# A per-token modulation repeated over rows: selection-matrix products against a store to DRAM and a strided read back

## The chip, the cores and the metric

The kernel runs on one core of a Trainium2 chip. The metric is the device time of one execution in microseconds; lower is better. Five engines work side by side: TensorE (PE, matrix products), VectorE (DVE), ScalarE (ACT), GpSimd (POOL) and SyncE (SP), which in this kernel only issues transfers. ACT issues transfers too, on a queue of its own. Engines wait for each other and for transfers through semaphores.

## The reference

Eight sequences of 1024 tokens with 512 channels go through two residual layers. The first is an adapter of rank 128 with a layer norm. The second is the one that matters here:

```
ctx    = causal_ema(x, tau_ctx)
gated  = x * sigmoid([x, ctx] @ Wg.T + bg)
h1     = gelu(x @ Wn1.T + bn1)
mod    = 0.5 + sigmoid(h1 @ Wn2.T + bn2)          # per token: D = 8 numbers
traces = [causal_ema(gated * mod[..., d], tau_d) for d in range(8)]
temporal = sum over d of traces[d] * softmax(blend)[d]
out    = (gelu(x @ Wsoma.T + b) * sigmoid(temporal @ Wtemp.T + b)) @ Wout.T
x      = x + layernorm(out)
```

The eight traces are decaying sums over time. Each scales the gated input of a token by one of the eight numbers `mod` of that token.

## The kernel before

The 8192 tokens are 16 tiles of 512 (`TOK`), each of four blocks `b` of 128 tokens. A program of slots runs over them: slot k finishes tile k-1 (its gates and output product), works on the middle of tile k, and begins tile k+1. Each engine's program is written out by hand in the order in which the engine runs it; only semaphores tie the engines together. A wait therefore holds everything behind it on that engine.

All large products are made three times with rounded operands (high times high, high times low, low times high), so PE has a great deal to do: L1026 is the line of these products.

The decaying sums inside a tile are made in spans of 32 tokens. For a block, `within_spans` (L1217 on PE) multiplies a table `Arep` with `U`, both with 128 partitions that stand for 32 tokens times four of the eight traces (NQ = 4; the two halves of the eight are `hh`, NH = 2). So `U` needs the gated input `g` with every token repeated on four partitions. [...] DVE then multiplies what was read by the blend weights (`products`, L902; 16 per tile, numbered 0 to 15 in the text). The first block waits for its four reads (`grep_in0`).

`Arep` (L962 on DVE) is the power of the decay times the modulation, so it needs the modulation repeated on the same partitions, `m_rep`: 16 spans times NH numbers on each partition. The modulation `m_nat` (L937, L588, L944) has a token per partition. Before the change it is repeated in three steps: PE multiplies it with a 0/1 selection matrix `spread` (`spread_modulation`, L1189; the matrix lies in `T_sb1`, which other data need in between, so SP loads it anew for each tile at L357); DVE keeps of each four columns the one that belongs to the partition by a product with `own` (L955) and a sum over four (L958). L911 is `gated`, which makes `g` ready.

The order around the change in one slot is, on PE: value gate 0, modulation, value gate 1, `spread_modulation`, value gates 2 and 3, half of a soma product, `within_spans` of block 0, and so on; on ACT: open gate 0, sigmoid of `m_nat`, store block 0, open gate 1, store block 1, and so on; on SP: load of the selection matrix, four output stores, `repeat_spans(0)` to `(3)`.

Of the kernel before, what the change touches and what calls it, by code (L numbers as in the profile page):

```python
# [4 lines left out]
P = 128  # L5
BATCHES, SEQ, C = 8, 1024, 512
# [34 lines left out]
def cond_resid_kernel(nc, x, xc, own, spread, ids, w1, w2, b1, b2, g0, be0, wg, wn1, wsoma, wtemp, wout, wn2,  # L41
# [10 lines left out]
    with ctx:  # L52
        def sb(name, shape, dt=F):
            return ctx.enter_context(nc.sbuf_tensor(name, shape, dt))
# [10 lines left out]
        def sem(name):  # L65
# [57 lines left out]
        m_all = U[:, 3, NI - 1, 96:96 + NI * NB * D].rearrange("p (y q) -> p y q", q=NQ)  # L123
# [6 lines left out]
        columns = sb("columns", [P, 11 + NQ])  # L130
        col, alpha_ctx, b1_col, own_q = columns[:, 0:9], columns[:, 9:10], columns[:, 10:11], columns[:, 11:11 + NQ]
# [8 lines left out]
        g_dram = nc.dram_tensor("g_blocks", [NB, P, C], F, kind="Internal").ap()  # L140
        x1_dram = nc.dram_tensor("x1_tiles", [2, P, NB * C], F, kind="Internal").ap()
# [31 lines left out]
        ld_spread = sem("ld_spread")  # L173
# [7 lines left out]
                 "m": 1, "mrep": 1, "S": 1, "Uused": PIECES // 2, "T": 4, "carry": 1}  # L181
# [22 lines left out]
        m_pre, m_ready, Bm_ready, mrep_ready, A_ready = sem("m_pre"), sem("m_ready"), sem("Bm_ready"), sem("mrep_ready"), sem("A_ready")  # L204
        mall_ready = sem("mall_ready")
# [85 lines left out]
        def _(sp):  # L291
# [26 lines left out]
            def first_loads():  # L318
# [5 lines left out]
                sp.dma_start(own_q, own).then_inc(ld_small, 16)  # L324
# [24 lines left out]
            def slot(k):  # L349
                has_prev, has_cur, has_next = parts_of(k)  # L350

                def load_spread():
                    if has_next:
                        sp.wait_ge(full["y"], upto(4, k + 1, NB - 1))
                    else:
                        sp.wait_ge(full["tt"], upto(4, k - 1, NB - 1))
                    sp.dma_start(T_sb1[:, :], spread).then_inc(ld_spread, 16)  # L357
# [16 lines left out]
                if has_prev:  # L374
# [11 lines left out]
                    if has_cur:  # L386
                        load_spread()
# [91 lines left out]
        def _(act):  # L479
# [6 lines left out]
            def slot(k):  # L486
# [95 lines left out]
                if has_cur:  # L582
# [44 lines left out]
            act.wait_ge(ld_small, 112)  # L627
# [14 lines left out]
        def _(dve):  # L642
# [16 lines left out]
            def small_tables():  # L659

                dve.wait_ge(ld_small, 112)
# [712 lines left out]
```

## Time and profile before

| | |
|---|---|
| Median of 3 runs | 1344.43 us (1341.11 to 1346.19) |
| The profiled execution | 1347.22 us, of which the span from first to last instruction is 1345.4 us |
| Busy share of ACT, POOL | 41%, 34% |
| Granted TensorE clock | 0.995 of full speed |
| Transfers | 190.41 MB in 93933 packets, a mean of 142 GB/s |
| Queue of ACT's transfers (q10) | 16.78 MB, 3.3% of 16 engines |

The profile counts an engine as busy while an instruction runs. Products on PE overlap, and their ends are modelled: a long row of them starts one each 0.227 us, though each is shown as 0.39 us. A busy PE is therefore no proof that PE is what the end waits for. "PEld" is PE's loading of weights. A row of the timeline is an instruction or several alike: its start, its length, its engine, its line, what it writes and reads, how many; in brackets the idle time before it and what ended that.

### The profile page before, as it was taken

To read this page: it belongs to the slowest core of one execution; us is meant where nothing else is said; L and a number is where in the kernel's file an instruction comes from. 1 tells how busy PE (TensorE), PEld (TensorE's weight loads), DVE (VectorE), ACT (ScalarE), POOL (GpSimd) and SP (SyncE) were. 2 spreads that over 40 slices of the span, in tenths; PEclk is the share of its full clock that TensorE was granted. 3 is DMA by queue.
4 is the path that set the end of the run, shared out by engine and by line. 5 is a ranking of instruction groups with operands and counts; after the bars stand their busy time and mean duration, and the time that the engine had idled before them with its cause. 6 is when DMAs were issued, how large, how long until landed. Compare 5 with 4: busy or idle time off the path is not lost.

```text
span 1345.4 us, 19282 instructions
## 1 busy us (share of the span) xinstructions
PE 1305.6 (97%) x7580; PEld 1015.1 (75%) x7580; DVE 1044.1 (78%) x1542; ACT 555.0 (41%) x892; POOL 460.9 (34%) x364
## 2 busy tenths in 40 slices
PE   4899999999999999999999999999999999999997
PEld 2668778687787878778687787878868787787766
DVE  7988777797778877787787778778687787778575
ACT  3426253343624525254252634426254262534422
POOL 3407144061521606135061531606125061431102
PEclk9899999999999999999999999999999999999999
DMA  7372442715336171352715425173342714325150
GB/s 269 141 241 81 153 161 71 258 40 183 137 105 218 55 244 62 128 196 80 239 40 179 173 86 204 48 235 118 118 165 78 256 66 164 149 86 181 40 181 32
DMA packets 93933, 190.41 MB, mean 142 GB/s; under 512 B 10258, under 2 KB 14994, under 8 KB 89746
## 3 DMA queue, kind: packets, MB, share of 16 engines
q1 hardware_dynamic: 84626, 172.39, 37.7%
q10 hardware_dynamic: 9216, 16.78, 3.3%
q8 instruction: 60, 0.98, 0.3%
q14 instruction: 31, 0.25, 0.1%
HBM read 138.81 MB, written 50.33 MB: 141 GB/s over the span
## 4 chain that ended last, share of the span: by engine, by line
PE 58%; DVE 16%; issue 9%; DMA 7%; ACT 4%; SPq 2%; POOL 1%; DVEq 0%; POOLq 0%
PE ring L1026 40%; DVE U_f L902 7%; PE Tp L1217 5%; DMA g_blocks<-g_f 4%; PE Tp L1026 3%; PE Tp L1228 3%; DMA grep<-g_blocks 3%; SPq L371 2%; DVE stats L837 2%; PE ring L1242 2%; ACT U_f L561 2%; DVE g_f L911 1%; DMA x<-g_blocks 1%; PE ring L1060 1%; PE ring L1063 1%
## 5 line engine op out<-in xcount | busy, mean ns | idle before, releaser
L425 POOL TENSOR_TENSOR Arep_r<-W,Arep_r 128x512 fp32r<-128x512 f32 x14 | 18.2, 1297 | 541.9 <-ACT Arep_r L524 541.9
L902 DVE TENSOR_TENSOR U_f<-grep,w_qs 128x1024 f32<-128x1024 f32 x128 | 150.8, 1220 | 49.2 <-issue 45.2
L571 ACT ACTIVATE g_f<-g_f 128x512 f32<-128x512 f32 x64 | 40.5, 632 | 260.7 <-DVE g_f L907 260.5
L1217 PE MATMUL Tp<-U_f,Arep_f 128*32 128x256 f32 x2048 | 130.0, 384 | 5.5 <-DVE U_f L902 5.3
L452 POOL TENSOR_TENSOR grep_f<-grep_f,beta_row 128x512 f32<-128x512 f32 x64 | 82.1, 1320 | 68.1 <-DMA grep_f<-x_tiles 68.1
L1217 PEld LDWEIGHTS Tp<-U_f,Arep_f 128*32 128x32 f32 x2048 | 56.1, 109 | 65.2 <-DVE U_f L902 23.0
L1026 PE MATMUL ring<-x1T_hi,Wsoma_hi 128*128 128x512 f32 x256 | 103.4, 404 | 0.0
L1026 PE MATMUL ring<-Wg_hi,x1T_hi 128*128 128x512 f32 x256 | 103.3, 403 | 0.0
L1026 PE MATMUL ring<-seq_hi,Wtemp_hi 128*128 128x512 f32 x256 | 101.0, 394 | 0.1
L1026 PE MATMUL ring<-Wout_hi,g_r 128*128 128x512 f32 x256 | 99.9, 390 | 1.1 <-DVE soma_r L758 1.0
L1026 PE MATMUL ring<-Wg_hi,x1T_lo 128*128 128x512 f32 x256 | 100.2, 392 | 0.0
L1026 PE MATMUL ring<-x1T_hi,Wsoma_r 128*128 128x512 f32 x256 | 100.2, 391 | 0.0
L1026 PE MATMUL ring<-x1T_lo,Wsoma_hi 128*128 128x512 f32 x256 | 100.0, 391 | 0.0
L907 DVE TENSOR_TENSOR g_f<-ring,bg_row 128x512 f32<-128x512 f32 x64 | 44.1, 689 | 71.9 <-PE ring L1026 71.6
L1026 PE MATMUL ring<-seq_hi,Wtemp_r 128*128 128x512 f32 x256 | 99.8, 390 | 0.0
L1026 PE MATMUL ring<-seq_lo,Wtemp_hi 128*128 128x512 f32 x256 | 99.8, 390 | 0.0
L1026 PE MATMUL ring<-Wout_hi,soma_r 128*128 128x512 f32 x256 | 99.7, 390 | 0.0
L1026 PE MATMUL ring<-Wg_r,x1T_hi 128*128 128x512 f32 x256 | 99.7, 390 | 0.0
L1026 PE MATMUL ring<-Wg_hi,seq_hi 128*128 128x512 f32 x256 | 99.7, 389 | 0.0
L1026 PE MATMUL ring<-Wout_r,g_r 128*128 128x512 f32 x256 | 99.7, 389 | 0.0
L1026 PE MATMUL ring<-Wg_hi,seq_lo 128*128 128x512 f32 x256 | 99.7, 389 | 0.0
L1026 PE MATMUL ring<-Wg_r,seq_hi 128*128 128x512 f32 x256 | 99.7, 389 | 0.0
(185 smaller groups left out, 3192.8 us busy)
## 6 DMA issues: line engine op xcount, KB each, us to landing
grep<-g_blocks SPq DMA_DIRECT2D x128, 256.0 KB, 3.7
grep_f<-in_xc SPq DMA_DIRECT2D x16, 1024.0 KB, 7.8
grep<-in_x SPq DMA_DIRECT2D x16, 1024.0 KB, 9.3
x_tiles<-x SPq DMA_DIRECT2D x16, 1024.0 KB, 6.9
g_blocks<-g_f ACTq DMA_DIRECT2D x64, 256.0 KB, 3.5
grep_f<-g_blocks SPq DMA_DIRECT2D x64, 256.0 KB, 3.5
x<-g_blocks SPq DMA_DIRECT2D x64, 256.0 KB, 3.9
grep_f<-x_tiles SPq DMA_DIRECT2D x16, 1024.0 KB, 4.8
```

Of the source, the lines that this page charges most:

```text
L371: sp.dma_start(spans_of(k, b)[q:P:NQ, :, :], g_dram[b].rearrange("(i s) c -> s i c", i=NI)).then_inc(spans_in(k, b)[0], 16)
L425: nc.gpsimd.tensor_tensor(W1_split[:, 1, :, :], W1[:, :, :], W1_split[:, 0, :, :].bitcast(F), ALU.subtract).then_inc(w1lo_ready, 1)
L452: nc.gpsimd.tensor_tensor(x1_back[:, b, :], x1_back[:, b, :], beta1_row[:, :], ALU.add).then_inc(x1b_ready, 1)
L561: nc.scalar.activation(res[:, b, :], res[:, b, :], ACT.Identity, scale=rstd1[:, b:b + 1]).then_inc(scaled_ready, 1)
L571: nc.scalar.activation(g[:, b, :], g[:, b, :], ACT.Sigmoid).then_inc(sig_ready, 1)
L837: V_.bn_stats(stats0[:, b, :], new[:, b, :]).then_inc(ln0_step, 1)
L902: V_.tensor_tensor(U[:, (n + 2) % 4, :, :], spans_of(k, b)[:, :, at], w_qs[:, hh, at].unsqueeze(1).to_broadcast([P, NI, HC]), ALU.mult).th ...
L907: V_.tensor_tensor(g[:, b, :], bank_of("wg", k, b)[:, :], bg_row[:, :], ALU.add).then_inc(pre_ready, 1)
L1026: last = nc.tensor.matmul(dst, lhsT(a, n), rhs(b, n), start=(first and n == begin and m == 0), stop=(final and n == steps - 1 and m == 2))
L1217: last = nc.tensor.matmul(Tp[b % 2][i * L:(i + 1) * L, at], Arep[:, b * NI + i, hh, :], U[:, (n + 2) % 4, i, :], start=(hh == 0 and c == 0 ...
L1228: last = nc.tensor.matmul(Tp[b % 2][:, :], Epow[a][rows, b, :], V[c][rows, :], start=False, stop=(m == 2))
L1242: last = nc.tensor.transpose(ps[:, n * P:(n + 1) * P], T_sb[b % 2][:, n * P:(n + 1) * P], ident[:, :])
```

## The change

The selection matrix, its reload per tile, the four products on it and the two DVE steps behind them are gone. Instead ACT stores `m_nat` to DRAM (`m_blocks`: 128 partitions, four pieces of 8 numbers, so 512 pieces of 32 bytes) behind the store of block 0 of `g`, and SP reads it back onto the partitions of `m_rep` (128 partitions, 16 pieces of 2 numbers, so 2048 pieces of 8 bytes), ahead of its reads of the spans. To keep the two numbers of a piece side by side, the eight traces are dealt out in another way over the partitions and the halves (`hh:D:NH` in place of `hh * NQ:(hh + 1) * NQ`, and the table of decays likewise).

```diff
@@ sync
-                def load_spread():
-                    if has_next:
-                        sp.wait_ge(full["y"], upto(4, k + 1, NB - 1))
-                    else:
-                        sp.wait_ge(full["tt"], upto(4, k - 1, NB - 1))
-                    sp.dma_start(T_sb1[:, :], spread).then_inc(ld_spread, 16)
+                def repeat_modulation():
+
+                    sp.wait_ge(m_stored, 16 * upto(1, k, 0))
+                    sp.dma_start(m_rep, m_dram.rearrange("x s (q h) -> (s q) x h", h=NH)).then_inc(ld_m, 16)
...
-                    if has_cur:
-                        load_spread()
                     for b in range(NB):
                         sp.wait_ge(res_ready, upto(4, k - 1, b))
                         sp.dma_start(out_tiles[k - 1, b * P:(b + 1) * P, :], res[:, b, :]).then_inc(stored, 16)
                 else:
                     second_loads()
-                    load_spread()
                 if has_cur:
+                    repeat_modulation()
                     for b in range(NB):
                         repeat_spans(b)
@@ scalar
                     store_spans(0)
+                    act.wait_ge(m_ready, upto(1, k, 0))
+                    if has_prev:
+                        act.wait_ge(ld_m, 16 * upto(1, k - 1, 0))
+                    nc.scalar.dma_start(m_dram.rearrange("(b i) s d -> (i s) b d", b=NB), m_nat).then_inc(m_stored, 16)
                     for b in range(1, NB):
                         open_gate(b)
                         store_spans(b)
@@ vector
                     gate_logits(1)
-                    dve.wait_ge(full["mrep"], upto(1, k, 0))
-                    V_.tensor_tensor(m_all, smp[:, 32:32 + NI * NB * D].rearrange("p (y q) -> p y q", q=NQ),
-                                     own_q.unsqueeze(1).to_broadcast([P, NI * NB * NH, NQ]), ALU.mult).then_inc(mall_ready, 1)
-                    dve.wait_ge(mall_ready, upto(1, k, 0))
-                    V_.tensor_reduce(m_rep.rearrange("p (b i) h -> p i b h", b=NB),
-                                     m_all.rearrange("p (i b h) q -> p i b h q", i=NI, b=NB), AX.X, ALU.add).then_inc(mrep_ready, 1)
                     gated(1)
-                    dve.wait_ge(mrep_ready, upto(1, k, 0))
+                    dve.wait_ge(ld_m, 16 * upto(1, k, 0))
                     V_.tensor_tensor(Arep[:, :, :, :],
@@ tensor
-                def spread_modulation():
-
-                    pe.wait_ge(m_ready, upto(1, k, 0))
-                    pe.wait_ge(ld_spread, 16 * upto(1, k, 0))
-                    for i in range(NI):
-                        last = nc.tensor.matmul(smp[:, 32 + NB * D * i:32 + NB * D * (i + 1)], T_sb1[:, i * P:(i + 1) * P],
-                                                U[:, 3, NI - 1, 0:NB * D], start=True, stop=True)
-                    last.then_inc(full["mrep"], 1)
...
                     pe.wait_ge(Bm_ready, upto(1, k, 0))
-                    pe.wait_ge(mrep_ready, upto(1, k, 0))
...
                     value_gate(1)
-                    spread_modulation()
                     value_gate(2)
```

On SP, in slot 1 from the load of tile 2's input to the reads of block 1, the program has these rows before (`out` is the kernel's output, `grep`, `grep_f` hold what `repeat_spans` reads, and what stands in brackets is what the row waits for):

```order
L308 DMA grep<-in_x 128x4x512 [waits U_ready]
L385 DMA grep_f<-x_tiles 128x2048 [waits h_full]
L357 DMA T_sb_f<-in_spread 128x512 [waits y_full]
L390 DMA out<-U_f 128x512 [waits res_ready] x4
L371 DMA grep<-g_blocks 32x4x512 [waits x1_ready,g_stored0]
L371 DMA grep<-g_blocks 32x4x512 x3
L371 DMA grep_f<-g_blocks 32x4x512 [waits g_stored1]
```

and these after (`U_f<-m_blocks` is the read back of the modulation; `m_rep` lies in a corner of `U`):

```order
L307 DMA grep<-in_x 128x4x512 [waits U_ready]
L381 DMA grep_f<-x_tiles 128x2048 [waits h_full]
L384 DMA out<-U_f 128x512 [waits res_ready] x4
L353 DMA U_f<-m_blocks 128x16x2 [waits m_stored]
L367 DMA grep<-g_blocks 32x4x512 [waits x1_ready,g_stored0]
L367 DMA grep<-g_blocks 32x4x512 x3
L367 DMA grep_f<-g_blocks 32x4x512 [waits g_stored1]
```

The load of the selection matrix ahead of the output stores is gone, and a new wait and a new read stand directly ahead of the four reads of block 0.

On DVE, in the same slot from the modulation's last step to the second product of block 0, the rows before are:

```order
L944 TENSOR_SCALAR U_f<-U_f 128x32 [waits msig_ready]
L948 TENSOR_TENSOR Bm<-U_f,Rpow 128x128 [waits m_ready]
L907 TENSOR_TENSOR g_f<-ring,bg_row 128x512 [waits wg_full]
L955 TENSOR_TENSOR U_f<-smp,columns 128x128 [waits mrep_full]
L958 TENSOR_REDUCE U_f<-U_f 128x4x4x2 [waits mall_ready]
L911 TENSOR_TENSOR g_f<-g_f,x_1 128x512 [waits sig_ready]
L962 TENSOR_TENSOR Arep_f<-U_f,Dpow 128x1024 [waits mrep_ready]
L902 TENSOR_TENSOR U_f<-grep,w_qs 128x1024 [waits last_kept,grep_in0,A_ready]
L907 TENSOR_TENSOR g_f<-ring,bg_row 128x512 [waits wg_full]
L902 TENSOR_TENSOR U_f<-grep,w_qs 128x1024
```

and after:

```order
L942 TENSOR_SCALAR U_f<-U_f 128x32 [waits msig_ready]
L946 TENSOR_TENSOR Bm<-U_f,Rpow 128x128 [waits m_ready]
L905 TENSOR_TENSOR g_f<-ring,bg_row 128x512 [waits wg_full]
L909 TENSOR_TENSOR g_f<-g_f,x_1 128x512 [waits sig_ready]
L954 TENSOR_TENSOR Arep_f<-U_f,Dpow 128x1024 [waits ld_m]
L900 TENSOR_TENSOR U_f<-grep,w_qs 128x1024 [waits last_kept,grep_in0,A_ready]
L905 TENSOR_TENSOR g_f<-ring,bg_row 128x512 [waits wg_full]
L900 TENSOR_TENSOR U_f<-grep,w_qs 128x1024
```

Two instructions are gone, and the table `Arep` waits for a transfer (`ld_m`) where it waited for DVE's own sum.

## Rows read from the trace of the kernel before

**Rows 1.** The page's busy time by engine: us (share of the span), instructions.

```profile
PE 1305.6 (97%) x7580; PEld 1015.1 (75%) x7580; DVE 1044.1 (78%) x1542; ACT 555.0 (41%) x892; POOL 460.9 (34%) x364
```

**Rows 2.** Waits between engines: waiter, awaited, us in total, times, longest.

```profile
DVE U_f L902 <- issue: 45.2, 16, 4.6
PEld Tp L1217 <- DVE U_f L902: 23.0, 41, 2.1
PE Tp L1217 <- DVE U_f L902: 5.3, 13, 1.6
```

**Rows 3.** Timeline of DVE in tile 9.

```profile
795.35 1.41 DVE L911 TENSOR_TENSOR g_f<-g_f,x 128x512 f32<-128x512 f32 x1 [1.32 <-ACT g_f L571]
796.68 0.17 DVE L944 TENSOR_SCALAR U_f<-U_f 128x32 f32<-128x32 f32 x1
...
800.25 0.29 DVE L955 TENSOR_TENSOR U_f<-smp,columns 128x128 f32<-128x128 f32 x1
800.57 0.29 DVE L958 TENSOR_REDUCE U_f<-U_f 128x32 f32<-128x128 f32 x1
...
801.43 1.22 DVE L962 TENSOR_TENSOR Arep_f<-U_f,Dpow 128x1024 f32<-128x1024 f32 x1
805.99 1.23 DVE L902 TENSOR_TENSOR U_f<-grep,w_qs 128x1024 f32<-128x1024 f32 x1 [3.33 <-issue]
...
818.33 1.22 DVE L902 TENSOR_TENSOR U_f<-grep_f,w_qs 128x1024 f32<-128x1024 f32 x1
...
824.91 4.62 DVE L902 TENSOR_TENSOR U_f<-x,w_qs 128x1024 f32<-128x1024 f32 x4
```

**Rows 4.** Timeline of PE in tile 9.

```profile
799.24 0.97 PE L1189 MATMUL smp<-U_f,T_sb_f 128*128 128x32 f32 x8
800.04 0.48 PE L1026 MATMUL ring<-Wg_hi,x1T_hi 128*128 128x512 f32 x1
...
812.51 1.93 PE L1217 MATMUL Tp<-U_f,Arep_f 128*32 128x256 f32 x32
...
828.14 2.08 PE L1217 MATMUL Tp<-U_f,Arep_f 128*32 128x256 f32 x32
```

**Rows 5.** Issue of ACT's store of block 0 in tile 9.

```profile
796.79 0.33 ACTq L567 DMA_DIRECT2D g_blocks<-g_f  x1
```

**Rows 6.** Issues of SP's reads of block 0 in tiles 0 and 9.

```profile
68.35 2.62 SPq L371 DMA_DIRECT2D grep<-g_blocks  x4
...
798.88 2.54 SPq L371 DMA_DIRECT2D grep<-g_blocks  x4
```

**Rows 7.** Transfers from 798.8 to 806.2 us: busy tenths in 40 slices.

```profile
DMA  0000000089779959987889745988889734300000
```

**Rows 8.** Timeline of DVE in tile 10 and the start of tile 11.

```profile
875.28 1.41 DVE L911 TENSOR_TENSOR g_f<-g_f,x 128x512 f32<-128x512 f32 x1 [0.89 <-ACT g_f L571]
...
905.31 4.62 DVE L902 TENSOR_TENSOR U_f<-x,w_qs 128x1024 f32<-128x1024 f32 x4
...
956.83 1.41 DVE L911 TENSOR_TENSOR g_f<-g_f,x 128x512 f32<-128x512 f32 x1 [1.37 <-ACT g_f L571]
```

**Rows 9.** Transfers from 2 to 2.5 us, small loads only: packets, MB, share.

```profile
q1 hardware_dynamic: 144, 0.01, 18.5%
```

**Rows 10.** The page's queue of SP: packets, MB, share of 16 engines.

```profile
q1 hardware_dynamic: 84626, 172.39, 37.7%
```

**Rows 11.** SP's issue of that load.

```profile
1.16 0.38 SPq L321 DMA_DIRECT2D V_hi_f<-in_taus  x1
```

**Rows 12.** Timeline of DVE in tile 14.

```profile
1209.09 1.23 DVE L902 TENSOR_TENSOR U_f<-grep,w_qs 128x1024 f32<-128x1024 f32 x1 [1.87 <-issue]
...
1222.89 1.21 DVE L902 TENSOR_TENSOR U_f<-grep_f,w_qs 128x1024 f32<-128x1024 f32 x1
```

**Rows 13.** The same products of the first tile.

```profile
74.94 1.23 DVE L902 TENSOR_TENSOR U_f<-grep,w_qs 128x1024 f32<-128x1024 f32 x1 [0.53 <-issue]
87.28 1.22 DVE L902 TENSOR_TENSOR U_f<-grep_f,w_qs 128x1024 f32<-128x1024 f32 x1
```

More of the change, by code:

```diff
@@ L38, with cond_resid_kernel @@
 ALS = 12
-def cond_resid_kernel(nc, x, xc, own, spread, ids, w1, w2, b1, b2, g0, be0, wg, wn1, wsoma, wtemp, wout, wn2,
+def cond_resid_kernel(nc, x, xc, ids, w1, w2, b1, b2, g0, be0, wg, wn1, wsoma, wtemp, wout, wn2,
                       bg, g1, be1, cols, taus, bn2, blend, eye, bits, out):
@@ L129, in cond_resid_kernel @@
         stats = sb("stats", [P, 16 * NB])
-        columns = sb("columns", [P, 11 + NQ])
-        col, alpha_ctx, b1_col, own_q = columns[:, 0:9], columns[:, 9:10], columns[:, 10:11], columns[:, 11:11 + NQ]
+        columns = sb("columns", [P, 11])
+        col, alpha_ctx, b1_col = columns[:, 0:9], columns[:, 9:10], columns[:, 10:11]
         Wn2 = sb("Wn2", [P, D])
@@ L140, in cond_resid_kernel @@
         g_dram = nc.dram_tensor("g_blocks", [NB, P, C], F, kind="Internal").ap()
+        m_dram = nc.dram_tensor("m_blocks", [NB * NI, L, D], F, kind="Internal").ap()
         x1_dram = nc.dram_tensor("x1_tiles", [2, P, NB * C], F, kind="Internal").ap()
@@ L172, in cond_resid_kernel @@
         ld_back = sem("ld_back")
-        ld_spread = sem("ld_spread")
+        m_stored, ld_m = sem("m_stored"), sem("ld_m")
         ld_w1, ld_w2, ld_b2, ld_norm = sem("ld_w1"), sem("ld_w2"), sem("ld_b2"), sem("ld_norm")
@@ L180, in cond_resid_kernel @@
         names = {"h": 1, "temp": 4, "n1": 1, "soma": 4, "trx": 4, "tt": 4, "out": 4, "y": 4, "wg": 4,
-                 "m": 1, "mrep": 1, "S": 1, "Uused": PIECES // 2, "T": 4, "carry": 1}
+                 "m": 1, "S": 1, "Uused": PIECES // 2, "T": 4, "carry": 1}
         full = {n: sem(f"{n}_full") for n in names}
@@ L625, in slot @@
                         x1_high(n)
-            act.wait_ge(ld_small, 112)
+            act.wait_ge(ld_small, 96)
             nc.scalar.activation(alpha[:, 0, :], alpha[:, 0, :], ACT.Exp).then_inc(setup_exp, 1)
@@ L659, in small_tables @@
             def small_tables():
-                dve.wait_ge(ld_small, 112)
+                dve.wait_ge(ld_small, 96)
                 link(V_.tensor_reduce(blend_s, blend_c, AX.X, ALU.max))
@@ L674, in small_tables @@
                         V_.tensor_copy(blend_x[:, hh, n, :].rearrange("p (s q) -> p q s", q=NQ),
-                                       blend_c[:, n, hh * NQ:(hh + 1) * NQ].unsqueeze(2).to_broadcast([P, NQ, L]))
+                                       blend_c[:, n, hh:D:NH].unsqueeze(2).to_broadcast([P, NQ, L]))
                 for n in range(NC):
@@ L1288, in slot @@
                         x1_by_channels(n)
-            pe.wait_ge(ld_small, 112)
+            pe.wait_ge(ld_small, 96)
             pe.wait_ge(blend_ready, 2)
@@ L1347 @@
     rows = np.arange(P)
-    tau_table = np.concatenate([taus[rows % D][:, None], taus[rows % NQ][:, None], taus[NQ + rows % NQ][:, None],
+    tau_table = np.concatenate([taus[rows % D][:, None], taus[NH * (rows % NQ)][:, None], taus[NH * (rows % NQ) + 1][:, None],
                                 np.broadcast_to(taus[None, :], (P, D)),
@@ L1354 @@
     arrays = {
-        "x": c(xs), "xc": c(xs.transpose(0, 2, 1)), "own": (rows[:, None] % NQ == np.arange(NQ)[None, :]).astype(np.float32),
-        "spread": (np.arange(NI * P)[None, :] // NQ == rows[:, None]).astype(np.float32),
-        "ids": np.asarray(itok_B_0_8).reshape(1, BATCHES),
+        "x": c(xs), "xc": c(xs.transpose(0, 2, 1)), "ids": np.asarray(itok_B_0_8).reshape(1, BATCHES),
         "w1": c(L0_cond_W1), "w2": c(L0_cond_W2), "b1": c(L0_cond_b1), "b2": each(L0_cond_b2),
```

5 lines of the change are left out of this document (1 added, 4 removed).

## The prediction

> **What bounds the kernel now.** I read the page's busy shares first. PE is busy for 97% of the span [rows 1], and a reader might stop there: PE is the bound, so PE work taken away is time won. The waits say otherwise. At L1217 PE and its weight loads wait for DVE's products, 28.3 us in 54 waits, and DVE's first product of a tile waits 45.2 us in 16 waits, one per tile, for something that the profile calls issue [rows 2]. So once per tile the end is set by something other than PE.
>
> The timelines of tile 9 show what. DVE makes gated block 0 ready at 796.76, ACT issues its store at 796.79, and SP, which waits for the store to land, issues the four reads of block 0 at 798.88 [rows 3, 5, 6]. The transfers begin in the ninth slice, at 800.28, and run nearly full until 805.3 [rows 7]. The first product starts at 805.99, after 3.33 us idle; its other input, the table of L962, was done at 802.65 [rows 3]. That wait is the landing of the reads. From there DVE goes on almost without a gap: product 7 ends at 819.55 and product 15 at 829.53 [rows 3]. PE takes up the last four products in a group that ends at 830.22, which is 0.69 us behind product 15 [rows 4], and it is 0.69 or 0.70 us in all 16 tiles. PE never arrives so late that the last product lies ready for it. From product 15 to the next tile's gated block 0 PE works without a stop, and that stretch is rigid: 829.53 to 876.69 is 47.2 us, and 909.93 to 958.24 is 48.3 us in the tile that also changes its adapter weights [rows 3, 8].
>
> A tile is therefore a closed loop: gated block 0 to first product, 9.23 us in tile 9 (store, reads); first product to product 7, 13.56; to product 15, 9.98; back to gated block 0, 47.2. I cost the change by what it does to each of these.
>
> **What is taken away.** On PE, four products on the selection matrix: they start at 799.24 and the next product starts at 800.04 [rows 4], 0.80 us a tile, 12.8 us in all. They stand between gated block 0 and the first product, where the end waits for transfers and not for PE, so they are worth nothing there. They are worth something only where PE is late for block 0. On DVE, two steps of 0.29 us [rows 3]. They lie in the stretch in which DVE then idles for 3.33 us; nothing. On SP, a load of 256 KB per tile that was done long before; nothing. If the cover of PE's 0.80 us were gone, that is, if the reads landed early, the whole 12.8 us would count.
>
> **What is added, in tile 9.** The modulation is ready at 796.85, before ACT has finished issuing its first store at 797.12 [rows 3, 5], so ACT does not wait; behind it is the gate of block 1, for which ACT idles anyway. The m store leaves at about 797.15. The g store took 2.09 us from its issue to SP's answer [rows 5, 6]. The m store comes 0.36 us later and has more, smaller pieces, 512 against 128. No row has a store of small pieces. A small load shows 144 packets at 18.5% of 16 engines over 0.5 us, 10.3 ns a packet [rows 9]; the mean packet of SP's queue, mostly 2 KB, is 37.7% of 16 x 1345.4 us over 84626, 96 ns [rows 10]. By these 32 pieces per engine take 0.33 us or 3.1 us. I take the small one, being the nearest kind, and let the store land 0.4 us after the g store.
>
> Then SP issues the read back. An issue costs SP 0.34 to 0.6 us (0.38 for a small load, a quarter of 2.54 for a span read) [rows 6, 11]; 0.5 with its step. Queued behind it on SP are the four reads of block 0, for which DVE waits, and the reads of the other blocks.
>
> Then the queue itself. The read back has 2048 pieces of 8 bytes, 128 per engine, and the span reads come behind them on the same queue. By the small packet they hold each engine 128 x 10.3 ns = 1.3 us, by the mean packet 12.3 us. Of this 0.5 us lies inside the start-up of the span reads (1.40 us from issue to first packet [rows 6, 7], their issue being 0.5 later than the read back's), so 0.8 us is added.
>
> The first product is later by 0.4 + 0.5 + 0.8 = 1.7 us. The ends: 0.8 us (rival B), and 0.4 + 0.5 + 11.8 = 12.7 us at the mean packet's price. The range keeps the low end; the high one is far from the nearest row, so I keep it only in part, as a rival. The table of L962 is no bound: with the read back landed about 802.2 it ends about 803.5, ahead of 807.7.
>
> **What is given back.** A later first product removes waits behind it. From first product to the end of product 7 it takes 13.56 us in tiles 0 and 9, but 15.01 in tile 14 [rows 3, 12, 13], where PE is later against DVE and DVE waits for it now and then. Summed over the 16 tiles (tile 0 is one end, tiles 14 and 15, 15.0 us each, the other) the excess over 13.55 is 7.3 us. With products 1.7 us later and PE 0.80 us earlier all of it goes.
>
> **The sum.** In the first tile the reads wait until 68.35 [rows 6] for a later input (`x1_ready`), and the m store and its read back pass in that time; there I count the queue alone, 0.7 us. 15 x 1.7 + 0.7 - 7.3 = 18.9 us. On the profiled execution, 1347.2 us, that is 1366.1; the median of the runs is 2.8 us lower, so 1363. The likeliest case alone spans 1.2 to 2.8 us per tile, 1356 to 1380.
>
> **Rivals.**
>
> A. PE is the bound, and its 12.8 us are won: 1344.4 - 12.8 = 1331.6. For it: 97% busy. Against it: the 0.69 us of every tile and the 16 waits of DVE. It would need the reads to land before DVE is free, and the change issues them later. The Trainium skill, page "Perfetto Trace Analysis", section "Identifying Performance Opportunities", says that improving a kernel generally means improving its most contended engine, found by occupancy. By that rule this rival would be first; it also warns that matmul busy share is a poor measure of PE's nearness to its limit, and the trace agrees with the warning.
>
> B. The new transfers cost their issue only. The read back moves 16 KB, and its pieces pass in the start-up of the span reads. Then the store lands 0.3 us later (so few bytes may land sooner) and the issue costs 0.5: 15 x 0.8 + 0.3 - 7.3 = 5.0 us, 1349.4, which is no change. The row of small packets would need to be at most 0.5 us / 128 = 4 ns a piece, less than half of what it shows. The Trainium skill, page "DMA: Bandwidth & Descriptors", section "Anatomy of one DMA", fits a transfer as about 2.0 us plus its bytes at 436 GB/s; by that rule 16 KB are an estimated 0.04 us of the queue and this rival holds.
>
> C. Small strided pieces are slow. The packets of rows 9 are eight to an engine; 128 to an engine from scattered places may run at four times their price, 40 ns, 5.1 us per read back. Then 0.4 + 0.5 + 4.6 = 5.5 us a tile: 15 x 5.5 + 0.7 - 7.3 = 76 us, 1420. It decides from about 3 us per tile upward. For it: nothing in the trace has such a transfer, and the store has 32-byte pieces too. Against it: 10.3 ns in the only rows near it.
>
> **How the numbers follow.** Something under 0.5% (6.7 us) can't be told from no change here. The forecast has a chance of 0.62, C 0.18, B 0.13, A 0.07. Slower by over 0.5%: forecast and C, 0.80. Same: B, and a little of the others, 0.13. Faster: A, 0.07. The low end of the range is B's, 1348. The high end, 1402, reaches to 4.3 us per tile, a part of C; above it I leave 0.12, below it 0.07.
>
> **What would show it.** The profile after should have the gap from SP's wait to its first span read about 0.9 us longer, the first product of a middle tile 10.5 to 11.5 us after gated block 0 where it was 9.2, about 1 us of new idle time before the table of L962 and about 4.2 us (3.33 before) between table and first product, and the stretch from product 15 to the next gated block unchanged at 47.2 and 48.3 us. DVE's waits for PE between the products should nearly vanish. If the first product is not later, the steps on SP and its queue are wrong; if it is more than 3 us later, the price of a piece is; if the loop's rigid stretch changes, the whole frame is. If PE's group at the end of the tile stops ending 0.69 us behind product 15, PE is the bound after all.

## The result and the profile after

The changed kernel takes 1360.09 us (median of 4 runs, 1355.98 to 1363.08), the kernel before beside it 1343.97 us (1341.11 to 1346.19). The ratio is 1.0119, with a 95% interval of 1.01 to 1.0138. The profiled execution took 1357.84 us, 10.62 more than the one of before.

The page after, busy time by engine:

```profile
PE 1297.8 (96%) x7452; PEld 1000.6 (74%) x7452; DVE 1037.1 (76%) x1510; ACT 555.1 (41%) x892; POOL 461.3 (34%) x364
```

PE does 7.8 us less than before and DVE 7.0 us less [rows 1], and still the kernel takes longer.

In what follows the span reads are SP's four reads of `g`'s block 0 (`repeat_spans`, L371 before, L367 after): ACT has stored the block to DRAM (`store_spans`), and each read brings it back onto every fourth partition, so that every token stands on four of them. The read back is SP's new read of the stored modulation.

Its queues of SP (q1) and ACT (q10), and the two new transfers (issuing engine, count, size, median us from issue to landing):

```profile
q1 hardware_dynamic: 115202, 168.46, 37.7%
q10 hardware_dynamic: 17664, 17.04, 3.6%
...
m_blocks<-U_f ACTq DMA_DIRECT2D x16, 16.0 KB, 2.1
U_f<-m_blocks SPq DMA_DIRECT2D x16, 16.0 KB, 2.8
```

SP's queue moves 3.9 MB less in 30,576 packets more, in the same share of its time [rows 10].

The waits after, DVE's and PE's at the products (rows of before: rows 2):

```profile
DVE U_f L900 <- DMA grep<-g_blocks: 48.1, 16, 4.2
DVE Arep_f L954 <- DMA U_f<-m_blocks: 6.8, 12, 1.6
```

```profile
PE Tp L1199 <- DVE U_f L900: 9.1, 26, 1.1
```

The first product still waits once in every tile for its reads; the table now waits too, but only a little.

Tile 9 after: ACT's issues, SP's issues, and DVE (the rows of before are rows 5, 6 and 3):

```profile
804.40 0.33 ACTq L561 DMA_DIRECT2D g_blocks<-g_f  x1
804.83 0.42 ACTq L591 DMA_DIRECT2D m_blocks<-U_f  x1
```

```profile
806.90 0.38 SPq L353 DMA_DIRECT2D U_f<-m_blocks  x1
807.38 4.58 SPq L367 DMA_DIRECT2D grep<-g_blocks  x4
```

```profile
802.97 1.40 DVE L909 TENSOR_TENSOR g_f<-g_f,x 128x512 f32<-128x512 f32 x1 [1.34 <-ACT g_f L565]
...
809.74 1.23 DVE L954 TENSOR_TENSOR Arep_f<-U_f,Dpow 128x1024 f32<-128x1024 f32 x1 [0.61 <-DMA U_f<-m_blocks]
815.12 1.22 DVE L900 TENSOR_TENSOR U_f<-grep,w_qs 128x1024 f32<-128x1024 f32 x1 [4.16 <-DMA grep<-g_blocks]
...
828.60 4.62 DVE L900 TENSOR_TENSOR U_f<-grep,w_qs 128x1024 f32<-128x1024 f32 x4
```

The store of the modulation leaves 0.43 us behind the store of g, SP gets its answer 2.07 us later, and the read back takes 0.48 us of SP. The first span read is issued 2.98 us after the issue of g's store; it was 2.09. The four issues themselves take longer too: 4.58 us here, the longest of all, and 2.9 to 3.5 in the other tiles but the first, where before had 2.54 in most [rows 6]; summed over the 16 tiles 50.7 us against 41.2. In tile 9 the first product starts 10.75 us after gated block 0 and was 9.23; over all 16 tiles the mean is 10.11 against 9.21.

I cut both profiled executions at the same five points of every tile and summed the differences over the 16 tiles (us against the profiled execution of before):

```
stretch                            changed kernel   its repeat
start, to gated block 0 of tile 0      + 2.91         + 2.88
gated block 0 to first product         +14.33         +15.41
first product to product 7             - 7.29         - 7.25
product 7 to product 15                + 0.62         + 1.73
product 15 to next gated block 0       + 0.05           0.00
total                                  +10.62         +12.76
```

The terms add up to the whole. The first row was in no step of the prediction. Two profiles of one kernel differ by over 1 us in the fourth row (1.2 for before, 1.1 for the changed one), so small differences there mean nothing. The difference of the medians, 16.1 us, is larger than that of this pair of profiled executions.

The trace has every piece of the read back as a packet. These are the transfers of tile 9 in the changed kernel, first from 807.9 to 809.3 us (packets, MB, share of 16 engines), then from 807.9 to 811.9 in slices of 0.1 us:

```profile
q1 hardware_dynamic: 2064, 0.02, 81.9%
```

```profile
DMA  1348999999951047357966899956595677999988
```

The 2064 packets hold the 16 engines for 81.9% of 1.4 us, 8.9 ns each. The 2048 pieces pass from 807.92 to 809.21, in 1.3 us, and the first packet of the span reads follows at 809.33. Over all 16 tiles a piece holds its engine for 8.7 ns in the mean; the first piece comes 1.0 us after SP's issue of the read back. The first packet of the span reads comes 1.93 us after their issue, where it was 1.38 in before, so it is 0.55 us later (0.51 in the repeat). But their last packet comes only 0.25 us later after the issue (0.34 in the repeat, 0.41 between the two repeats): from first packet to last the reads take a little less than before.

### The profile page after: what moved, and what is told of

The parts are those of the page before. It is cut to its first block, busy times and chain, and to the rows that moved or that the text cites. A ratio compares the mean times of both kernels' runs of the same rounds, so it can differ in the third digit from the quotient of the medians.

```text
span 1356.0 us, 19008 instructions
## 1 busy us (share of the span) xinstructions
PE 1297.8 (96%) x7452; PEld 1000.6 (74%) x7452; DVE 1037.1 (76%) x1510; ACT 555.1 (41%) x892; POOL 461.3 (34%) x364
## 4 chain that ended last, share of the span: by engine, by line
PE 36%; DVE 24%; issue 12%; DMA 11%; ACT 6%; SPq 4%; POOL 3%; ACTq 0%; DVEq 0%; POOLq 0%
PE ring L1018 21%; DVE U_f L900 11%; DMA grep<-g_blocks 5%; SPq L367 4%; PE Tp L1199 3%; PE Tp L1210 3%; PE Tp L1018 3%; ACT U_f L555 3%; DVE stats L835 3%; DVE g_f L909 3%; DMA m_blocks<-U_f 2%; DMA g_blocks<-g_f 2%; DMA x<-g_blocks 2%; PE ring L1224 2%; POOL rows L462 1%
```

## The experiments

All times are medians; ratios are to the kernel before, run beside on the same chip. "The loop" is the sum of the four lower rows of the table above.

**The same two kernels again.** No edit.

> The changed kernel once more, beside the three below. In its profile the loop from gated block 0 to the first product was 0.9 us longer per tile, of which 0.71 us is SP issuing its span reads later (11.4 us over 16 tiles) and 0.18 us what comes behind that issue (2.9 us in all), the waits between the products were 7.3 us shorter in all, and the first tile began 2.9 us later. Theory L (the loop): ratio to before 1.010 to 1.013 again, with the same parts. If the late start of the first tile is chance, it is not there again and the span is about 1353; if it belongs to the change, tile 0's gated block is again near 68.0.

1362.31 us, ratio 1.0128 (1.011 to 1.0147), profiled execution 1359.98.

> The kernel before once more, for its start. Its one profile has tile 0's gated block ready at 65.1 us; the five profiles of changed kernels have it at 66.9 to 68.8. If the later start belongs to the change (the initial loads are one fewer, and each lands at another time), it is 65 again; if it is chance of the start-up, it is anywhere from 65 to 69. Ratio 1.000 within 0.2%. The loop (sum over 16 tiles of gated block 0 to first product, 147.4 us) should repeat within 3 us.

1344.17 us, ratio 0.9999 (0.9988 to 1.001), profiled execution 1344.22. Gated block 0 of tile 0 is at 65.14 and 63.10 us in the two profiles of before and at 68.05 and 68.02 in those of after. Between the two repeats the difference is 15.76 us: 4.92 of start and 10.84 of loop. The later start comes with the change; the experiment on the start below says why.

**The transfers and their wait left out.** The table is made from a constant 1, so the modulation enters neither table nor result of the in-span sums.

```diff
-                    act.wait_ge(m_ready, upto(1, k, 0))
-                    nc.scalar.dma_start(m_dram..., m_nat).then_inc(m_stored, 16)
-                    sp.wait_ge(m_stored, 16 * upto(1, k, 0))
-                    sp.dma_start(m_rep, m_dram...).then_inc(ld_m, 16)
-                    dve.wait_ge(ld_m, 16 * upto(1, k, 0))
-                                     m_rep.unsqueeze(3)
+                                     m_const.unsqueeze(2).unsqueeze(3)
```

> Leaves out the repeated modulation: no m store, no read back, the table of the spans is made from a constant 1. What is left is the change's saving alone (the products on the selection matrix, two DVE steps and the matrix's load are gone). Theory L: PE's 12.8 us are worth only the waits between products in the tiles in which PE is late: 4 to 7 us, 1337 to 1341, ratio 0.995 to 0.998. Rival P (PE is the bound): all 12.8 us, ratio 0.990 or below.

1344.26 us, ratio 0.9997 (0.9984 to 1.0011). With all the removals and none of the additions the kernel is not faster; I had expected 1337 to 1341 us. Rival A, which wanted 12.8 us, is dead. In its profile gated block 0 to first product is 2.85 us shorter over all tiles, the next stretch 4.26 shorter, product 7 to 15 1.38 longer, the start 1.77 later. So the removals aren't worth nothing in the loop: it is 5.7 us shorter than in the profiled execution of before and 4.7 shorter than in its repeat, and the later start (1.8 and 3.8 us) takes part of that back.

**The store and SP's wait kept, the read back left out** (table from a constant).

```diff
                     sp.wait_ge(m_stored, 16 * upto(1, k, 0))
-                    sp.dma_start(m_rep, m_dram...).then_inc(ld_m, 16)
```

> Leaves out the read back; the m store and SP's wait for it stay, and the table of the spans is made from a constant 1. no_transfers was 0.9997 of before, after_again 1.0128. Theory L splits the difference into SP's wait for the m store (its later landing, about 0.45 us a tile), the issue of the read back (about 0.43 us a tile) and its pieces (0.2 to 0.4 us a tile). The wait alone: SP's span reads 0.45 us later per tile than in no_transfers, 1349 to 1352, ratio 1.003 to 1.006. Rival W (the wait for the store is the whole cost, issue and pieces are hidden): ratio 1.010 or above. Rival Q (only the read back costs): 1.000.

1351.28 us, ratio 1.0054 (1.0037 to 1.0071). This is within what I had expected. The stretch to the first product is 5.49 us longer than before (0.34 per tile), against 14.33 with the read back.

**The read back in 128 pieces of 128 bytes** in place of 2048 of 8 (the numbers come to the wrong partitions).

```diff
-                    sp.dma_start(m_rep, m_dram.rearrange("x s (q h) -> (s q) x h", h=NH))
+                    sp.dma_start(U[:, 3, NI - 1, 64:64 + NB * NI * NH],
+                                 m_dram.rearrange("x s d -> (x s d)").rearrange("(p f) -> p f", p=P))
```

> The read back takes the same 16 KB as 128 contiguous pieces of 128 bytes in place of 2048 of 8 (the numbers land on the wrong partitions). Wait and issue stay. Theory L with the sizes of the profile: the pieces cost 0.18 us a tile or less, so 1 to 3 us less than after_again. With the size of the prediction (0.8 us a tile for the pieces): 12 us less than after_again, ratio to before about 1.003. Rival C (small pieces are slow): more than that.

1358.06 us, ratio 1.009 (1.0076 to 1.0105): 4.3 us less than the repeat of the changed kernel, where the prediction's size of the queue would have given 12 less, and a little more than the 1 to 3 that I expected. Its stretch to the first product is 8.84 us longer than before, so the 1920 pieces more that the change has cost 5.5 us (6.6 by the repeat); counted only from SP's issue of the first span read on, 4.3 (5.5). That is 0.27 to 0.41 us per tile, or 2.2 to 3.4 ns for each of the 120 pieces more per engine. This is what reaches the first product, not what a piece costs: in the trace a piece of 8 bytes holds its engine for 8.7 ns, and one of 128 bytes, 8 to an engine, for 12.4 ns. The read itself landed 1.6 us after its issue, not 2.8. Behind 128 pieces the span reads' first packet comes 1.46 us after their issue in the mean, behind 2048 pieces 1.93. SP's issues are longer behind the many pieces too: behind a read of 128 pieces its four span issues took 42.0 us over the 16 tiles, behind one of 2048 50.7, in before 41.2. About half of these 8.7 us reaches the first product. By the Trainium skill, page "DMA: Bandwidth & Descriptors", section "Anatomy of one DMA", bytes at 436 GB/s and a fixed part make the price. The fit there is for transfers that GpSimd issues, and both forms here, issued by SP, move 16 KB, so that rule has no term for the difference. The same page's section "Why small descriptors are slow (HBM only)" has one, some 3 cycles a packet beside one per 32 bytes; 4 cycles at the 850 MHz of its section "Specifications" would be an estimated 4.7 ns for one of 8 bytes. The measured 8.7 ns is nearly twice that, and the measurement decides.

**The read back behind the reads of block 0.**

```diff
-                    repeat_modulation()
-                    for b in range(NB):
+                    repeat_spans(0)
+                    repeat_modulation()
+                    for b in range(1, NB):
```

> SP's read back stands behind the four reads of block 0 in place of ahead of them. Theory L: the span reads are issued 2.09 us after the g store as before, but the read back leaves 2.5 us later and lands behind them, and the table (1.22 us on DVE) comes only then, so the first product is 2.2 to 3 us later than in the kernel before, not 1: ratio 1.022 to 1.030, 1375 to 1386. A theory by which only the span reads' issue counts would give 0.998 to 1.003.

1391.54 us, ratio 1.0339 (1.0317 to 1.0362), above the 1375 to 1386 that I had expected. SP issues the span reads as early as before, and the table then waits for a read that stands in the queue behind 1 MB. DVE in tile 9:

```profile
835.24 1.22 DVE L955 TENSOR_TENSOR Arep_f<-U_f,Dpow 128x1024 f32<-128x1024 f32 x1 [6.00 <-DMA U_f<-m_blocks]
836.50 1.23 DVE L901 TENSOR_TENSOR U_f<-grep,w_qs 128x1024 f32<-128x1024 f32 x1
```

The read back lands 5.3 us after its issue here (median), and 2.8 in front of the span reads. In front it costs the span reads 0.2 to 0.4 us a tile; behind them it waits for them, and the stretch to the first product is 40.9 us longer than before over the 16 tiles.

**The read back issued by ACT, on ACT's queue.**

```diff
-                    sp.wait_ge(m_stored, 16 * upto(1, k, 0))
-                    sp.dma_start(m_rep, m_dram...).then_inc(ld_m, 16)
...
                     nc.scalar.dma_start(m_dram..., m_nat).then_inc(m_stored, 16)
+                    act.wait_ge(m_stored, 16 * upto(1, k, 0))
+                    nc.scalar.dma_start(m_rep, m_dram...).then_inc(ld_m, 16)
```

> The read back is issued by ACT on its own queue, behind a wait for the m store, in a time in which ACT idles; SP's span reads wait for the g store alone again. Theory L: SP issues the span reads 2.09 us after the g store as before, the first product stands 9.2 us after gated block 0 or earlier, and PE's 0.8 us per tile shortens the waits between the products by 4 to 7 us in all: 1337 to 1341 us, ratio 0.995 to 0.998 (1341 to 1344 if the late start belongs to the change). Rival D (the small pieces cost wherever they are issued, because they share the 16 engines with the span reads): the first product stays 0.5 to 1 us later, 1352 to 1358. Rival P (PE is the bound): 1331 to 1333, ratio 0.990.

1343.93 us, ratio 0.9982 (0.9959 to 1.0004). All of the loss is gone, with gated block 0 of tile 0 still as late as 68.55. Waits of DVE in this kernel:

```profile
DVE Arep_f L955 <- DMA U_f<-m_blocks: 31.5, 16, 2.8
DVE U_f L901 <- DMA grep<-g_blocks: 11.3, 9, 2.4
```

The roles are changed: the table waits for its read, 2.0 us a tile, and in most tiles the first product starts 0.03 us behind the table. The read takes longer than on SP's queue:

```profile
U_f<-m_blocks ACTq DMA_DIRECT2D x16, 16.0 KB, 4.6
```

Gated block 0 to first product is 6.36 us shorter than before over all tiles. The first product also comes sooner after SP's issue, 6.5 us in the mean (6.2 in most tiles) where it was 6.8. Leaving the transfers out didn't bring that (6.8 too). The packets offer a reason. In before ACT's store of block 1 of `g` is issued 2.7 us after the span reads, its first packet comes 4.25 us after their issue, and it shares the 16 engines with the rest of them; their last packet comes at 6.4 (medians of 16 tiles). Here the same store is issued as early but stands behind the read back on ACT's queue: its first packet comes at 5.2, and the last of the span reads already at 5.7. No run holds that store back by itself, so this is read from the traces and not shown by an experiment.

**The modulation ready and stored ahead of g.** Its last addition is made on ACT, so that the store doesn't wait for DVE; SP reads back ahead of the spans as in the change.

```diff
                     nc.scalar.activation(m_nat, m_nat, ACT.Sigmoid).then_inc(msig_ready, 1)
+                    nc.scalar.activation(m_nat, m_nat, ACT.Identity, bias=half).then_inc(m_ready, 1)
+                    nc.scalar.dma_start(m_dram..., m_nat).then_inc(m_stored, 16)
...
                     store_spans(0)
-                    nc.scalar.dma_start(m_dram..., m_nat).then_inc(m_stored, 16)
```

> The last step of the modulation (plus 0.5) moves from DVE, where it stands behind the gated product, to ACT, directly behind the sigmoid, and the m store goes out ahead of the g store; SP's read back stays ahead of its span reads. Theory L: the m store leaves about 1.4 us earlier and has landed before the g store has, SP issues the read back while it would wait for the g store, and the span reads leave on time; the table is ready as before. What is left of the cost is the pieces at most: 1341 to 1346, ratio 0.997 to 1.001, against 1.0128. Rival D (the pieces share the engines with the span reads, wherever they start): 1350 and more.

1351.04 us, ratio 1.0048 (1.0031 to 1.0066). The time is a miss: I had expected 1341 to 1346, and it lies where rival D put it, at 1350 and more. But what rival D says, that the first product stays late, isn't so. SP's first span read is issued as early as before, and of the 14.33 us to the first product 1.56 are left. SP's issue alone gave back 12.3 us: 11.4 later than before over all tiles in the change, 0.9 earlier here. In its profile the loop is 3.3 us shorter than before and the start, which I had not counted, 4.45 us later. The read back is issued 1.3 us ahead of the span reads here, not 0.48, and their four issues take 2.5 to 2.7 us again in 13 of the 16 tiles.

**Both: early store, read back by ACT.**

```diff
-                    sp.dma_start(m_rep, m_dram...).then_inc(ld_m, 16)
+                    nc.scalar.dma_start(m_rep, m_dram...).then_inc(ld_m, 16)
```

> The modulation's last addition on ACT, its store ahead of the store of g's block 0, and the read back issued by ACT on its own queue (no small load put back). act_read's wait of the table for the read was 2.4 us per tile and its span reads were free: with m stored 0.4 to 0.9 us earlier and the read back queued behind the g store, theory 1 (the table's wait for the read is what the first product waits for) gives the table 0.5 to 1 us earlier per tile, 8 to 15 us in the sum from gated block 0 to product 0, less what PE then takes as bound: 1336 to 1342. Rival: the g store, now behind the m store, lands 0.3 to 0.5 us later and the spans take over as the bound: 1343 to 1349.

1348.74 us, ratio 1.0012 (0.9976 to 1.0048). A miss: I had expected 1336 to 1342. The time is at the upper end of the rival's range, but not for its reason: the store of `g` lands no later, SP issues the span reads 2.12 us after gated block 0 in most tiles as in before. The table no longer waits (0.5 us in the sum), but the first product comes 6.3 to 7.1 us after SP's issue in most tiles, as in before, and waits for its reads as there. The gain to the first product is 1.16 us over all tiles, not 8 to 15. The read back passes before the span reads here and no longer holds up the store of block 1: that store's first packet comes 4.3 us after SP's issue, as in before, and the short reads of the version with ACT's read back are gone with it. The start is later still, 71.11.

**The start.** The load of `own` was one of eight small loads ahead of the large load of tile 0's input. The experiment puts a load of the same size in its place, into columns that nothing reads.

```diff
+                sp.dma_start(columns[:, 11:15], eye[:, 0:4]).then_inc(ld_small, 16)
                 sp.dma_start(ident[:, :], eye).then_inc(ld_small, 16)
...
-            act.wait_ge(ld_small, 96)
+            act.wait_ge(ld_small, 112)
```

> The changed kernel with one small load put where the load of own stood: 128 pieces of 16 bytes, into columns that nothing reads, waited for as own was. Nothing else differs. Theory S: the later start (first gated block at 68.0 us in place of 63.1 to 65.1) comes from the missing small load, which lets SP issue the large load of tile 0's xT 0.5 us earlier and sends it in among the small ones; with it back bn2_row lands 2.6 to 2.8 us after its issue, DVE's first instruction is at 6.6 to 6.7, the first h product at 12.6, the first gated block at 63 to 65.5, and the time falls by 2.5 to 4.5 us to 1356 to 1360 (ratio 1.008 to 1.010). Theory T, the start is later for another reason (the other order of blend_x, the store that ACT waits on): the first gated block stays at 67 to 70 and the time at 1360 to 1363.

1357.96 us, ratio 1.0095 (1.0061 to 1.0129): in step with theory S, but the interval is too wide to tell 3 us from none. Its profiled execution, 1361.81 us, is even 4 us longer than that of the changed kernel, with the start 4.8 us earlier but product 7 to 15, which the edit doesn't touch, 6.1 us longer; no run gives a reason for that. So the gain in time isn't shown by this run; what the traces show is the start itself. SP's issue of the last small load, and ACT's first instruction that waits for it, in the changed kernel:

```profile
3.47 0.43 SPq L325 DMA_DIRECT2D bn_row<-in_bn  x1
```

```profile
7.55 0.21 ACT L627 ACTIVATE V_hi_f<-V_hi_f 128x12 f32<-128x12 f32 x1 [5.52 <-DMA bn_row<-in_bn]
```

and with the load put back:

```profile
3.94 0.43 SPq L326 DMA_DIRECT2D bn_row<-in_bn  x1
```

```profile
6.61 0.21 ACT L628 ACTIVATE V_hi_f<-V_hi_f 128x12 f32<-128x12 f32 x1 [4.58 <-DMA bn_row<-in_bn]
```

Issued 0.47 us later, the last small load lands 0.94 us earlier: 2.7 us after its issue, not 4.1. Behind it DVE makes the tables of the decays, and more of them now fall into the time of POOL's first work. DVE in the changed kernel:

```profile
15.12 0.29 DVE L704 SCALAR_TENSOR_TENSOR g_f<-g_f 128x128 f32<-128x128 f32 x1
...
15.59 1.34 DVE L704 SCALAR_TENSOR_TENSOR g_f<-g_f 128x128 f32<-128x128 f32 x1
16.85 1.21 DVE L705 SCALAR_TENSOR_TENSOR V_hi_f<-V_hi_f 128x1 f32<-128x1 f32 x1
...
18.18 1.24 DVE L704 SCALAR_TENSOR_TENSOR g_f<-g_f 128x128 f32<-128x128 f32 x1
19.34 1.22 DVE L705 SCALAR_TENSOR_TENSOR V_hi_f<-V_hi_f 128x1 f32<-128x1 f32 x1
...
22.24 0.68 DVE L761 TENSOR_TENSOR T_sb_r<-ring,T_sb_r 128x512 fp32r<-128x512 f32 x1
```

POOL in the same kernel:

```profile
15.51 5.03 POOL L433 TENSOR_TENSOR x<-grep,b_row 128x512 f32<-128x512 f32 x4 [14.67 <-DMA grep<-in_x]
```

and DVE with the load put back:

```profile
15.32 1.26 DVE L706 SCALAR_TENSOR_TENSOR V_hi_f<-V_hi_f 128x1 f32<-128x1 f32 x1
...
18.94 0.69 DVE L762 TENSOR_TENSOR T_sb_r<-ring,T_sb_r 128x512 fp32r<-128x512 f32 x1 [0.60 <-ACT T_sb_r L496]
```

Once POOL is at work an instruction of 0.15 to 0.29 us takes 1.2 to 1.3 us, four times in the one kernel and once in the other. That POOL is the reason is read from the times: POOL's four instructions in the changed kernel, 1.26 to 1.31 us each, end at 16.78, 18.05, 19.27 and 20.54, and the four slow ones of DVE end at 16.93, 18.07, 19.42 and 20.56. So 0.94 us late at 7 us have become 3.3 at 22, and gated block 0 is at 63.22 with the load and at 68.05 without.

How many of DVE's small instructions fall into POOL's time tells where gated block 0 of tile 0 lies, in all 14 traces (us):

```
slow instructions   gated block 0 of tile 0
0                   62.98, 63.10
1                   63.22
2                   65.14, 65.19
3                   66.91
4                   68.02, 68.05, 68.55, 68.84
5                   68.81
6                   69.59, 70.08, 71.11
```

The nine kernels without the small load (the changed one and its repeat among them) have 3 to 6, the three with it put back (two of them below) 0 to 2, and the two traces of before 2 and 0: that is their difference of 2 us. The late landing isn't all of it. In the version without the transfers the last small load landed at 6.37 us, as early as in before, and three instructions were still caught, because POOL, whose own load had landed early too, began at 14.75 us and not at 15.08 or 15.86. Why the small load lands later when issued earlier is open: the large load is issued 0.47 us behind it in both.

**The same load put back where ACT reads.** The edit is that of the last experiment on the version with ACT's read back.

> The same small load put back in act_read, where ACT issues the read back on its own queue. Theory S: first gated block at 63 to 65.5 in place of 68.55, and 3 to 4.5 us less than act_read's 1343.9: 1339.5 to 1341, ratio 0.995 to 0.997, the first version under the kernel before. Theory T: 1343 to 1345, ratio 0.998 to 1.0.

1341.07 us, ratio 0.9978 (0.9942 to 1.0014), profiled execution 1338.19. The interval is too wide to choose between the theories by the time. Gated block 0 of tile 0 is at 62.98, as theory S has it, and the loop is 0.8 us from that of the version without the load.

**The modulation stored by SP, read back by ACT.** SP idles there, waiting for g's store.

```diff
+                    sp.wait_ge(m_ready, upto(1, k, 0))
+                    sp.dma_start(m_dram..., m_nat).then_inc(m_stored, 16)
...
-                    nc.scalar.dma_start(m_dram..., m_nat).then_inc(m_stored, 16)
                     act.wait_ge(m_stored, 16 * upto(1, k, 0))
                     nc.scalar.dma_start(m_rep, m_dram...).then_inc(ld_m, 16)
```

> As act_read_pad (small load put back, read back issued by ACT), but the modulation's store is issued by SP, beside ACT's issue of the store of g's block 0 instead of 0.4 us behind it. In act_read_pad the table waits 31.0 us in the sum for the read back and directly behind it stands the first product. Theory 1, the table's wait is the bound of the first product: the store lands 0.4 us earlier in each tile, so 6 us less from gated block 0 to product 0, of which half may be handed on to PE; with the profiled execution of act_read_pad at 1338: 1332 to 1336, ratio 0.991 to 0.995. Rival: the spans (12.4 us of waits in the sum still) or PE take over at once: 1337 to 1341, ratio 0.995 to 0.998. Rival 2: the store's issue on SP lies ahead of the span reads and pushes them by its 0.4 us where SP is late: 1342 or more.

1339.53 us, ratio 0.9966 (0.9953 to 0.9979), profiled execution 1336.47. This is the one version whose whole interval lies under the kernel before, by 4.3 us (0.3%). SP's issues in tile 9, and DVE's wait:

```profile
790.78 0.38 SPq L356 DMA_DIRECT2D m_blocks<-U_f  x1
792.87 2.54 SPq L370 DMA_DIRECT2D grep<-g_blocks  x4
```

```profile
DVE Arep_f L955 <- DMA U_f<-m_blocks: 31.2, 16, 2.8
```

The store costs the span reads nothing: they are issued 2.2 us after gated block 0 in most tiles (2.1 in before). But the table waits as long as it did (31.2 us against 31.0): the store takes 2.4 us from SP and took 2.1 from ACT, and of the 0.4 us per tile that I expected 0.13 arrived (2.0 us over all tiles). The time falls into the first rival's range, but not for its reason: the table came hardly earlier, so little was there to be handed on. The loop is 3.9 us shorter than in the last version, but 2.6 of it lie in product 7 to 15, which the edit doesn't touch.

## Why the prediction came out right, and where it was wrong

The forecast was 1363 and the result 1360.1, on the right side and by the right frame, but that the two are only 3 us apart is in part luck. For the profiled execution the forecast was 1366.1, and it took 1357.84. The medians lie closer because the profiled execution of before was 2.8 us above its median and the one of after 2.3 below its own. And two errors partly cancelled. By the sum the loop should have cost 18.9 us; it cost 7.7 (10.8 between the two repeats). The start should have cost nothing and cost 2.9 (4.9 between the repeats).

- **The frame**: the loop of four stretches, with the rigid one from product 15 to the next gated block. Right. That stretch changed by 0.05 us in 743, and the last product group still ends 0.69 us behind product 15 in every tile.
- **Removals worth nothing but where PE is late**: right for the kernel as a whole (0.9997 without the transfers). In the loop they are worth about 5 of PE's 12.8 us; 4.3 of them are waits of DVE among the first eight products, and 2.3 come from SP, which issues its span reads earlier, above all in tiles 2 and 11. The load of the selection matrix, which I had put at nothing, may be behind the latter; no run keeps it alone.
- **Store lands 0.4 us later, issue 0.5 us**: right where nothing else holds SP. Its first span read is 0.88 us later in most tiles. In before it was late already in three of the fifteen tiles that I counted, and the sum is 11.4 us and not 13.5. Without the issue 5.49 us of the 14.33 remained, and with both taken out of SP's way 1.56.
- **The price of a piece, 10.3 ns, 1.3 us for 128**: right. The pieces hold their engines for 8.7 ns each and pass in 1.3 us.
- **The queue adds 0.8 us per tile**: this is the term that was wrong. From SP's issue to the first product it is 0.18 us per tile (0.26 in the repeat, 0.36 between the two repeats), 2.9 us over all tiles (5.7 between the repeats) where the sum has 12.7. Two things make the difference. I had let 0.5 us of the pieces pass in the start-up of the span reads, taking the 1.40 us from issue to first packet for both; the read back's first piece comes after 1.0 us, so 0.85 us of them pass there and the span reads begin 0.55 us later. And of these 0.55 us only a part arrives, since the span reads make up 0.1 to 0.3 us on their way. Rival B had said that it needed less than 4 ns a piece. It didn't get that, and in the loop its 5.0 us was still nearer than the forecast's 18.9: a cost in the queue isn't the same as a cost at what waits behind it. The 0.04 us of the queue that stand beside rival B were 1.3 us when measured.
- **The first tile, 0.7 us**: 0.2, for the same reason.
- **Given back, 7.3 us**: 7.29, and 7.2 to 7.25 in the repeat and in four further kernels with a later first product. That part was exact, since it is bounded by the excess that before shows.
- **The start**: missed. I counted the removed small load of `own` at nothing. The two profiles of before differ by 2 us there, so one profile alone would not have shown it; two against two did, and the load put back brought the early start again in three kernels of three.
- **What would show it**: about 0.9 us more at SP's issue came as forecast, and so did the end of DVE's waits among the first eight products, which now take 13.55 us in all 16 tiles. The first product came 10.1 us after gated block 0 in the mean, below the 10.5 to 11.5 forecast. The time between table and first product was 3.4 us in the mean, not 4.2 (3.0 in before): the queue term again. The wait of the table was 0.4 us in the mean (6.8 over 16), not 1, though the read back landed 2.8 us after its issue, about as I had counted.

Not settled: whether the store of block 1 alone makes the difference where ACT reads back, and why an earlier large load goes with a later landing of a small one that was issued ahead of it. I did not try two read backs per tile, which would price issue and pieces once more.

## What to carry to other kernels

While a round trip through DRAM closes the loop, little of the work removed from a 97% busy engine shows (here about 5 of 12.8 us in the loop, and nothing in the whole); look for what each tile waits for once. A transfer added in front of that round trip on the same issuing engine costs its wait and its issue, here 0.9 us in most tiles; issued by another engine, or early enough, it cost none of that, and put behind the large reads it waited for them (47 us in all). What a transfer costs in the queue (1.3 us here) isn't what it costs the end (0.2 to 0.4): subtract what passes in the start-up of the next one. And a load that is removed changes when everything behind it lands: compare the start before the loop as its own term.

## What the runs showed of the hardware that I had not expected

- A read of 2048 pieces lengthened the issue of the four reads directly behind it on the same engine from 2.54 us to between 2.9 and 3.5 (once 4.6); one of 128 pieces did not, nor did the 2048 in most tiles when they were issued 1.3 us ahead.
- A piece of 8 bytes held its DMA engine for 8.7 ns, one of 128 bytes for 12.4 ns. 2048 pieces of 8 bytes take 2.8 us from issue to landing, 128 of 128 bytes 1.6 us.
- The same read of 2048 pieces lands after 2.8 us on SP's queue ahead of the span reads, after 4.6 on ACT's queue beside them, and after 5.3 behind them.
- A small load issued 0.47 us earlier, with the same loads ahead of and behind it but one, landed 0.94 us later.
- DVE instructions of 0.15 to 0.29 us lasted 1.2 to 1.3 us while POOL worked on 128x512 tiles, and ended 0.02 to 0.15 us behind one of POOL's.
